# Six instead of seven GpSimd products in a selective-scan and expert-lookup kernel, with new stage slots and VectorE sums for the last batches

## The reference

```python
x = x + mamba(LN(x))          # 256 inner channels, 16 states, then a small feed-forward block and a layer norm
x = x + experts(LN(x))        # 8 heads; per head one of 1024 row pairs is picked by a product-key search
x = x + gated_ssm(LN(x))      # 16 states, sigmoid gates, tanh, an output projection and a layer norm
x = x + experts(LN(x))        # the same weights as above
```

```python
def step(h, t):                       # 512 steps, for 256 channels x 16 states of each batch
    dA = exp(d_t[:, :, None] * A);  h = dA * h + (d_t * u_t)[:, :, None] * B_t[:, None, :]
    y_t = einsum('bdn,bn->bd', h, C_t)
# experts: for each token and head, one index, then
h = gelu(x . w_down[index]) * relu(score);   out = sum over heads of h * w_up[index]
```

## Time and profile before

| | us |
|---|---|
| median of 3 runs | 1947.96 |
| lowest and highest of them | 1942.91, 1949.53 |
| the profiled execution | 1943.8 |
| its span, first to last instruction | 1942.1 |
| VectorE busy | 1682.8 (87%) |
| TensorE busy | 1575.4 (81%) |
| ScalarE busy | 1553.1 (80%) |
| GpSimd busy | 1360.2 (70%) |

### The profile page before, as it was taken

The page is one execution under the profiler, slowest core; times in us unless marked ns, Lnnn a source line. Parts: engine busy times, 40 slices in busy tenths (PEclk is TensorE's granted clock), DMA queues, the critical chain, the costliest instruction groups (busy, mean ns, idle before and its releaser), DMA issues. The chain is left out here.

```text
span 1942.1 us, 24817 instructions
## 1 busy us (share of the span) xinstructions
PE 1575.4 (81%) x6097; PEld 874.6 (45%) x6186; DVE 1682.8 (87%) x4204; ACT 1553.1 (80%) x3287; POOL 1360.2 (70%) x1209
## 2 busy tenths in 40 slices
PE   5778788879898987888888988888888987776463
PEld 2333344435454544455444544455444544443342
DVE  3899989999999999999999999999999999944331
ACT  5666677879898988899888988899898987656543
POOL 0444647387887877787868877787868877777765
PEclk8899999999999999999999999999999999898776
DMA  6111202022323223232323232232323222233332
GB/s 152 49 55 30 68 26 73 20 82 79 102 82 90 82 79 97 71 98 80 101 69 98 82 90 85 71 100 80 95 71 101 83 85 81 79 116 107 95 95 84
DMA packets 84510, 159.45 MB, mean 82 GB/s; under 512 B 21097, under 2 KB 47105, under 8 KB 84289
## 3 DMA queue, kind: packets, MB, share of 16 engines
q0 software_dynamic: 49152, 134.28, 24.0%
q1 hardware_dynamic: 33952, 23.04, 4.0%
q10 hardware_dynamic: 1248, 0.34, 0.1%
HBM read 149.20 MB, written 8.39 MB: 81 GB/s over the span
## 5 line engine op out<-in xcount | busy, mean ns | idle before, releaser
L1481 POOL DMA_INDIRECT rows<-in_experts,index x1024 | 983.7, 961 | 357.8 <-issue 293.6
L1365 DVE TENSOR_TENSOR_SCAN hp<-dA,fed_ps 128x1024 f32<-128x1024 f32 x256 | 583.1, 2278 | 8.2 <-issue 5.5
L795 PE MATMUL ysum<-hp,ident 128*128 128x512 f32 x1024 | 478.5, 611 | 20.1 <-DVE hp L1375 12.2
L1496 POOL TENSOR_TENSOR hp<-hp,c_row 128x1024 f32<-128x1024 f32 x112 | 264.7, 2364 | 166.2 <-ACT c_row L1055 156.7
L1038 ACT ACTIVATE dA<-delta,decay 128x511 f32<-128x511 f32 x512 | 334.7, 712 | 18.8 <-issue 16.5
L1349 DVE TENSOR_TENSOR fed_ps<-du,b_ps 128x1024 f32<-128x1024 f32 x256 | 313.3, 1224 | 32.9 <-PE b_ps L770 21.5
L1017 ACT ACTIVATE rows<-rows,coef 128x128 f32<-128x128 f32 x1024 | 310.8, 391 | 14.3 <-DVE coef L1285 14.0
L1278 DVE CUSTOM_DVE_ANT_0 rows<-rows,xn 128x128 f32<-128x128 f32 x1024 | 254.1, 310 | 61.9 <-DMA rows<-in_experts,index 61.5
L795 PEld LDWEIGHTS ysum<-hp,ident 128*128 128x128 f32 x1024 | 200.3, 197 | 234.0 <-issue 193.0
L945 ACT ACT_TABLE_LOAD x229 | 293.8, 1283 | 9.0 <-PEq L547 5.0
L728 PE MATMUL bank<-rows,ident 128*128 128x256 f32 x1024 | 247.4, 397 | 23.3 <-ACT rows L1017 23.3
(11 more groups left out here) (182 smaller groups left out, 2143.4 us busy)
## 6 DMA issues: line engine op xcount, KB each, us to landing
rows<-in_experts,index POOLq DMA_INDIRECT x1024, 2.7
x_in<-in_x SPq DMA_DIRECT2D x16, 256.0 KB, 4.7
rows<-in_x SPq DMA_DIRECT2D x16, 256.0 KB, 5.1
x_shifted<-rows SPq DMA_DIRECT2D x16, 256.0 KB, 2.0
x_res<-x_shifted SPq DMA_DIRECT2D x16, 256.0 KB, 4.8
y<-x SPq DMA_DIRECT2D x16, 256.0 KB, 3.0
rows<-in_taps SPq DMA_DIRECT2D x1, 512.0 KB
rows<-in_wq_t SPq DMA_DIRECT2D x1, 512.0 KB, 5.0
```

The lines of the kernel that those rows point to most:

```text
L795: mm = nc.tensor.matmul(ysum[:, j, :], ident[:], hp[:, BUFFER[k], j, :], start=(k == SUM_ORDER[0]), stop=(k == SUM_ORDER[-1]))
L1365: nc.vector.tensor_tensor_scan(flat, dA[:, n % NDA, :, :].rearrange("p a b -> p (a b)"), fed_ps[:].rearrange("p a b -> p (a b)"), 0.0, ALU ...
L1481: pool.indirect_dma_start(e.rows[:, t, h, :], None, A["experts"], bass.IndirectOffsetOnAxis(ap=e.index[:, t, h:h + 1], axis=0)).then_inc(e ...
L1496: pool.tensor_tensor(state, state, c_row[:, k % NCR, :].unsqueeze(1).to_broadcast([P, NH, T]), ALU.mult).then_inc(pool_read, 1)
```

## The change

Three things change, and every other line stays.

First, `POOL_STATES` loses state 13: VectorE multiplies that state by C from PSUM, ScalarE no longer copies its C row, and its product is summed one slot group earlier.

Second, `SLOTS` and `LAST_SLOTS` get new numbers for most stages. Those of VectorE and GpSimd follow in full, before and after, since the argument uses them; the rest of the tables moves in the same manner, by a few slots (`LAST_SLOTS` of the A and B stages by up to 15).

Third, for the last batches (`in_tail`: batch 15 in e1; batches 13, 14 and 15 in e2) ScalarE's scaling, TensorE's sum and ScalarE's copy are left out. `pile_rows` does the same on VectorE, in place in the residual tile, right behind `experts_weigh`. What used `x2` of batch 15 uses `x1` of it, and a fetch behind a piled batch waits for `added` in place of `summed`.

```diff
-POOL_STATES = (1, 3, 5, 7, 9, 11, 13)
+POOL_STATES = (1, 3, 5, 7, 9, 11)
+TAIL_E2 = 13
+def in_tail(site, m):
+    return isinstance(m, int) and m >= (NB - 1 if site == 1 else TAIL_E2)
...
+            def pile_rows(e, n, half, dst, residual):
+                dve.wait_ge(e.weighed, at(n, 2, half))
+                first = NB - 1 if e is e1 else TAIL_E2
+                done = ((n - first) * 2 + half) * HALF * HEADS
+                for h in range(HEADS):
+                    for t in range(half * HALF, (half + 1) * HALF):
+                        src = (residual if h == 0 else dst)[:, t, :]
+                        if h:
+                            dve.wait_ge(e.piled, done + h * HALF + t % HALF - 1)
+                        op = nc.vector.scalar_tensor_tensor(out=dst[:, t, :], in0=e.rows[:, t, h, P:2 * P],
+                                                            scalar=e.coef[:, t, h:h + 1], in1=src, op0=ALU.mult,
+                                                            op1=ALU.add)
+                        op.then_inc(e.piled, 1)
+                dve.wait_ge(e.piled, done + HALF * HEADS)
+                dve.sem_inc(e.added, 1)
...
             def experts_sum(e, k, i, m, stage, half, residual):
+                if in_tail(e.site, m):
+                    return
...
             def experts_scale(e, m, t):
+                if in_tail(e.site, m):
+                    return
...
                     for m, r, k in due("dve_weigh_e2", i, q, slot):
                         experts_weigh(e2, m, k)
+                        if in_tail(2, m):
+                            pile_rows(e2, m, k, x3[r], x3[r])
...
-                    if later(n):
+                    if in_tail(e.site, n) and in_tail(e.site, n - 1):
+                        pool.wait_ge(e.added, at(n - 1, 2, t // HALF))
+                    elif later(n):
                         pool.wait_ge(e.summed, at(n - 1, 2, t // HALF))
```

```diff
 SLOTS
-    "dve_dot_e1": (POST, (60, 63, 78, 80)),      "dve_dot_e2": (POST, (209, 220, 236, 240)),
+    "dve_dot_e1": (POST, (51, 63, 73, 80)),      "dve_dot_e2": (POST, (214, 220, 227, 237)),
-    "dve_weigh_e1": (POST, (66, 84)),            "dve_weigh_e2": (POST, (225, 244)),
+    "dve_weigh_e1": (POST, (67, 87)),            "dve_weigh_e2": (POST, (225, 242)),
-    "dve_index_e1": (POST, (42, 52)),            "dve_index_e2": (POST, (183, 197)),
+    "dve_index_e1": (POST, (40, 58)),            "dve_index_e2": (POST, (184, 195)),
-    "pool_delta": (PRE, (57,)),                  "pool_x3": (POST, (132,)),
+    "pool_delta": (PRE, (50,)),                  "pool_x3": (POST, (139,)),
-    "pool_fetch_e1": (POST, (36, 46, 51, 53, 63, 64, 66, 69)),
+    "pool_fetch_e1": (POST, (37, 43, 46, 55, 57, 60, 65, 73)),
-    "pool_fetch_e2": (POST, (195, 195, 206, 209, 214, 218, 221, 221)),
+    "pool_fetch_e2": (POST, (185, 193, 204, 206, 211, 217, 222, 223)),
 LAST_SLOTS
-    "dve_top_e2": (POST, (168, 175, 181, 189)),  "dve_index_e2": (POST, (179, 205)),
+    "dve_top_e2": (POST, (155, 166, 183, 186)),  "dve_index_e2": (POST, (174, 191)),
-    "dve_dot_e2": (POST, (197, 222, 237, 243)),  "dve_weigh_e2": (POST, (235, 244)),
+    "dve_dot_e2": (POST, (206, 212, 237, 243)),  "dve_weigh_e2": (POST, (217, 244)),
-    "dve_scan_b": (POST, (123,)),                "pool_x3": (POST, (121,)),
+    "dve_scan_b": (POST, (121,)),                "pool_x3": (POST, (129,)),
-    "pool_fetch_e1": (POST, (42, 43, 47, 48, 53, 64, 67, 73)),
+    "pool_fetch_e1": (POST, (29, 36, 38, 46, 47, 56, 60, 66)),
-    "pool_fetch_e2": (POST, (189, 189, 202, 210, 215, 219, 221, 230)),
+    "pool_fetch_e2": (POST, (173, 196, 199, 203, 206, 214, 218, 221)),
```

More of the change, by code:

```diff
@@ L136 @@
[L136 to L147 removed]
+    "dve_top_e1": (POST, (36, 39, 44, 48)),
@@ L214 @@
-    "pool_fetch_e2": (POST, (189, 189, 202, 210, 215, 219, 221, 230)),
+    "pe_out": (POST, (4,)),
+    "pe_ff1": (POST, (9,)),
+    "pe_ff2": (POST, (10,)),
+    "pe_ln_a": (POST, (15,)),
+    "pe_turn_e1": (POST, (27,)),
+    "pe_sim_e1": (POST, (29, 32, 37, 42)),
+    "pe_flip_e1": (POST, (32, 46)),
+    "pe_code_e1": (POST, (36, 46)),
+    "pe_sum_e1": (POST, (83, 89)),
+    "pe_turn_b": (POST, (113,)),
+    "pe_xp": (POST, (114,)),
+    "pe_gate": (POST, (115,)),
+    "pe_y": (POST, (122,)),
@@ new lines @@
+    "pe_z": (POST, (128,)),
+    "pe_ln_c": (POST, (129,)),
+    "pe_turn_e2": (POST, (142,)),
+    "pe_sim_e2": (POST, (146, 158, 182, 185)),
+    "pe_flip_e2": (POST, (171, 189)),
+    "pe_code_e2": (POST, (173, 193)),
+    "pe_sum_e2": (POST, (232, 248)),
+    "act_out": (POST, (11,)),
+    "act_gelu": (POST, (11,)),
+    "act_rstd_a": (POST, (15,)),
+    "act_rstd_e1": (POST, (22,)),
+    "act_norm_e1": (POST, (22,)),
+    "act_turn_e1": (POST, (26,)),
+    "act_flip_e1": (POST, (36, 47)),
@@ new lines @@
+    "act_gelu_e1": (POST, (58, 82)),
+    "act_scale_e1": (POST, (70, 70, 83, 83)),
+    "act_out_e1": (POST, (85, 86)),
+    "act_rstd_b": (POST, (105,)),
+    "act_norm_b": (POST, (111,)),
+    "act_turn_b": (POST, (111,)),
+    "act_xp": (POST, (114,)),
+    "act_gate": (POST, (120,)),
+    "act_tanh": (POST, (125,)),
+    "act_rstd_c": (POST, (131,)),
+    "act_rstd_e2": (POST, (136,)),
+    "act_norm_e2": (POST, (140,)),
+    "act_turn_e2": (POST, (146,)),
+    "act_flip_e2": (POST, (173, 194)),
@@ L215 @@
+    "dve_x3": (POST, (132,)),
+    "dve_stats_e2": (POST, (135,)),
+    "dve_shift_e2": (POST, (136,)),
+    "dve_top_e2": (POST, (155, 166, 183, 186)),
+    "dve_index_e2": (POST, (174, 191)),
+    "dve_dot_e2": (POST, (206, 212, 237, 243)),
+    "dve_weigh_e2": (POST, (217, 244)),
+    "pool_x3": (POST, (129,)),
+    "pool_fetch_e1": (POST, (29, 36, 38, 46, 47, 56, 60, 66)),
+    "pool_fetch_e2": (POST, (173, 196, 199, 203, 206, 214, 218, 221)),
 }
@@ L1167, in iteration @@
                     for m, r, k in due("act_out_e1", i, q, slot):
-                        if k == 0 and later(m):
+                        if k == 0 and later(m) and not in_tail(1, m):
                             act.wait_ge(x3_done, at(m - 1, 1))
```

221 lines of the change are left out of this document (89 added, 132 removed).

## The result

The changed kernel takes 1958.3 us (median of five runs, 1952.7 to 1966.1), the kernel before 1943.8 beside it; the ratio is 1.0084 [1.0061, 1.0106]. I had forecast 1924 and a range of 1904 to 1950. The profiled execution of after takes 1957.27 us, its span is 1955.5.

The account below looks back on a forecast made before the run. VectorE was taken to set the pace until the scans end, GpSimd in the tail. From 1943.8, -7 for the core and -17 for the tail gave 1919.8, forecast as a median of 1924 us, range 1904 to 1950.

Parts of the forecast that it names:

- ScalarE loses a copy and GpSimd 2.4 us a turn, neither of which is the bound; I count them at nothing, and no cover is lost: Moving state 13's product to VectorE frees time on ScalarE and GpSimd; counted as no gain and no loss.
- The price of state 13, 1.47 us: VectorE's cost for state 13's product: 1.13 us plus 0.34 for neighbouring scans, in each of 16 turns, 23.5 us.
- the stalls: VectorE steps held by GpSimd products, 1.7 us a plain turn, 5.5 behind the jump; partly gone, -0.8 a turn net.
- nothing remains: Lower bound in the turns, all stalls gone: a plain turn -0.2 us, one behind a jump -4.0, mean -2.1.
- Core -7, from -24 to +8: Scan turns before the tail: -10 us over turns 3 to 15, +3 for the first three, between the stall bounds.
- Turn 15: GpSimd's queue in turn 15: 17 fetch parts, six products and a `pool_x3`, 101 us, so they fit.
- Rival (3): GpSimd products hold VectorE dots behind scans of states 5 and 7: core +54, tail -14, 1988 us; chance 0.18.
- The end: Last fetch's end to kernel's end: 16 sums on VectorE take 4.7 us, gaining 5.8, so about 10.7 us remain.
- GpSimd's idle time in the tail: Two waits for an index of expert 2, 9.8 us together, go; 2 us left for batch 15's first index.
- The new queue: GpSimd's tail work: 160 fetches and three `pool_x3`, 204.5 us against 206.9, so 2.4 less; sums were not to stretch fetches.
- the sum of the tail, 217.2: Time behind the scans: 204.5 + 2 + 10.7 us, a gain of 16.6, between 12 and 19.

Follow-up runs that it names:

- e1: The kernel before with state 13's product moved from GpSimd to VectorE and nothing else; 1992.45 us, ratio 1.0266.
- e2: The changed kernel with seven products on GpSimd again, new slots and VectorE sums kept; 1954.08 us, ratio 1.0054 to the kernel before.
- e8: The changed kernel with spare matmuls in TensorE's gaps, at the turn's start and ahead of rest and dt; 1930.70 us, ratio 0.9939 to the kernel before.
- e5: The kernel before, old turns and seven products kept, with the changed kernel's `LAST_SLOTS` and sums on VectorE; 1936.01 us, ratio 0.9966.
- e18: e8 with every fourth tail sum waiting for the one right before it, so VectorE briefly runs empty; 1927.98 us, ratio 0.9901 to the kernel before.
- e19: e8 with every tail sum waiting for the one right before it; 1930.60 us, ratio 0.9925 to the kernel before.
- e3: The changed kernel with the last batches' sums on ScalarE and TensorE again; 1963.21 us, ratio 1.0123 to the kernel before.
- e17: e8 with VectorE's sums for batch 15 alone, expert 2 of batches 13 and 14 back on ScalarE and TensorE; 1930.37 us, ratio 0.9943 to the kernel before.
- e4: The kernel before, its slots and seven products kept, with only the last batches' sums on VectorE; 1943.94 us, ratio 1.0005.
- e16: The changed kernel with a spare 90-column sum ahead of each VectorE tail sum but the last 16; 1975.44 us, ratio 1.0169 to the kernel before.

## Why the prediction was wrong, point by point

- **"ScalarE loses a copy and GpSimd 2.4 us a turn, neither of which is the bound; I count them at nothing, and no cover is lost".** This step failed. I read TensorE's 94 busy of 105 us as room, and looked at what the change does to VectorE and GpSimd only. The sum had no term for TensorE. It gets a gap of 1.7 to 2.6 us at the start of ten of the turns 4 to 14, which needs the moved product (e1, e2), and gaps of 1.28 and 1.07 us ahead of rest and dt, which come with the slots of ScalarE's and TensorE's stages. Behind them TensorE runs at 1.2 GHz, 78.5 us in turns 4 to 14, and VectorE waits for `b_ps` and the code matmuls. The spare matmuls give 28 us back: the distance between 1930.7 and 1958.3. Why ScalarE is late with `xnbT` once the product has moved, I haven't followed further.
- **The price of state 13, 1.47 us, and the stalls.** In turns 4 to 14 they would give 11 x 1.47 = +16.2 us. Of the stalls I gave back 0.8 us a turn net of price and had "nothing remains" as the bound; it is the bound that came true. Held instructions fall from 45.3 us over the kernel to 3.8, and one sum of the tail, held by `pool_x3`, adds 1.5. In turns 4 to 14 they are 34.6 us before and 1.0 after, so VectorE's busy time should move by 16.2 - 33.6 = -17.4; it moved by -17.3. The size of the term was off, in the good direction. It is a term of VectorE's busy time alone, and what was saved there didn't reach the turn.
- **Core -7, from -24 to +8.** It was +25.0, outside. With the clock held (e8) the scans' part ends at 1704.6 for 1708.3 before, so -3.7: near my term by luck, since errors cancel. The start and turns 1 to 3 gave 5.9 us where I had them cost 3, turn 15 costs 5.4 more than before, and turns 4 to 14 give 3.2. In these the stalls gave more than I took, but VectorE's idle time in turns 4 to 14 is 54.9 us even then, 17.4 over before's 37.5. I had costed none of that: in a plain turn 1.4 us for `b_ps`, 0.9 for `rs`, 0.4 for the code matmuls; behind the jump about 2 for `dA`.
- **Turn 15.** I said that seventeen parts fit on GpSimd, and they do; but VectorE waits for the code matmuls there, and the turn takes 5.1 us more. The same turn was 114.0 us in e5, 116.4 in e8, 119.1 in e18 and 111.6 in e19, so its length hangs on how the steps fall, and I haven't settled on what.
- **Rival (3)** had the right mechanism in the wrong kernel. GpSimd's multiplies onto VectorE's steps is what the moved product does to the old order, +49 us in all (e1) and +44.6 up to the tail, where I had +54; with the new slots it doesn't come. That the changed kernel was slower is no merit of this rival: nothing of its stalls is in it. I had looked at the slots as a shift of VectorE's and GpSimd's queues, and did not ask what else they move.
- **The end.** Last fetch's end at 1945.3 to 1955.5 is 10.2 us, forecast 10.7, before 16.5; 16 sums take 4.29 us where I took 4.7 and the four multiply-adds of the earlier trace rows gave 4.2. Right.
- **GpSimd's idle time in the tail.** Gone, as forecast: 0.6 us of waiting for indices where the earlier trace rows has 3.7 and 6.1. e3 and e17 show that the sums remove one wait of over 6 us, e4 that they remove none without the new order.
- **The new queue and the sum of the tail, 217.2.** 160 fetches were left, as counted, and two `pool_x3` where I had three, but the tail is 222.2. I had held, by the Trainium skill ("SBUF — State Buffer", who interferes with whom), which marks it as inferred, that writing descriptors does not need what a VectorE instruction with two SBUF inputs locks, and so that sums and fetches pass each other. The dots bear that out: fetches beside them take 0.98 us in the mean and 1.10 at most in after. The sums don't: a fetch of 0.95 us lasts up to 2.85, 3.36 in e8 and 6.00 in e16. With those 7.4 us, 217.2 + 7.4 - 1.3 for the third `pool_x3` - 2 for batch 15's first index, which GpSimd didn't wait for, - 0.5 at the end + 0.6 of idle time is 221.4, of 222.2.

## What to carry to other kernels

When a schedule is moved, look for the gaps that the new order opens on every engine, not only on the one that sets the pace: here TensorE was busy for 95 of 108 us, and stretches at 1.2 GHz followed its gaps of 1 to 3 us, each 3.4 us of them worth 1.2 to 1.7 us of the turn. Read the granted clock turn by turn, since gaps as long stood in the kernel before without a stretch. Spare matmuls in such a gap can buy the clock back, but only where it is a true gap; in the old order the same ones cost 43 us, and the clock fell with them. A load that is taken off an engine moves everything behind it on that engine's queue, so price the meetings anew before you count the saving (e1).

## What the runs showed of the hardware that I had not expected

- An unbroken chain of 16 `scalar_tensor_tensor` instructions with both tensors in SBUF, 0.26 us apart, holds a GpSimd indirect DMA until 0.82 us behind its last one (six of after's seven chains), though not the first one to three fetches of the chain. Moments in which VectorE runs empty, three in 16 instructions, let the fetches through at 0.94 to 1.09 us (e18). Dots, which alternate with an accumulator read, hold none in after. Chains of 32 sums of two widths, as unbroken, held a fetch to their end once in seven (e16).
- A short VectorE step that begins ahead of a GpSimd multiply can be held by it all the same: the index step of e1 begins 0.63 us before the multiply and ends with it. A fetch's descriptors were being written when it began; what holds the step until the multiply begins isn't shown.
- The stretches at half clock lasted 3.4 to 10.2 us in turns 4 to 14 and were not the same from turn to turn, so that the same code took 108.0 us in one plain turn and 111.6 in another. The length of a turn alone says nothing of the schedule until the clock stands beside it.
